# Decoder, cross-attention and FFN on one core: merged maxima, a later context load, and MLP tiles ahead of the context turn

## The reference, cut to what matters

```python
for i in range(4):                                   # decoder layers, x is 8 x 256 x 256
    x = x + self_attention(layer_norm(x), Wq, Wk, Wv, Wo, bo)   # 4 local softmax heads, 4 causal linear heads
    h = layer_norm(x)
    x = x + gelu(h @ W1 + b1) @ W2 + b2
x = _layernorm(x_in + x)
# cross-attention to ctx (8 x 120 x 256): the mask leaves query i only key i, so the softmax is 1 at that key
x = _layernorm(x + (ctx row i, or the mean row past 120) @ Wv @ Wout + bout)
# FFN with composed weights: W = sum over the top 32 of 64 pairs of w_k * A_k @ B_k
x = _layernorm(x + gelu(x @ W1c) @ W2c)
```

## Time and profile before

| | us |
|---|---|
| median of 3 runs (lowest to highest) | 958.88 (958.85 to 959.15) |
| the profiled execution's own time | 958.88 |
| its span | 957.0 |
| PE busy | 944.3 (99%) |
| DVE busy | 672.8 (70%) |
| ACT busy | 612.4 (64%) |
| POOL busy | 480.0 (50%) |

### The profile page before, as it was taken

One profiled execution on the slowest core, in us unless ns is written; L12 is line 12 of the kernel. 1 busy time (PEld: TensorE's weight loads), 2 busy tenths in 40 slices (PEclk: granted clock), 3 DMA queues, 4 the chain that ended last, 5 costly groups with the idle time before them and its releaser, 6 DMA issues.

```text
span 957.0 us, 21341 instructions
## 1 busy us (share of the span) xinstructions
PE 944.3 (99%) x8394; PEld 815.4 (85%) x8394; DVE 672.8 (70%) x1531; ACT 612.4 (64%) x1387; POOL 480.0 (50%) x381
## 2 busy tenths in 40 slices
PE   7999999999999999999999999999999999999998
PEld 4687888888888889888888888888997889998997
DVE  7696868677677868696777668776662676766445
ACT  3777777786867867777778676786856345444220
POOL 3437365456836472776466366816247224006453
PEclk9999999999999999999999999999999999999999
DMA  6221000001110000021000002000028597720001
GB/s 211 88 91 45 2 17 2 4 15 51 40 45 18 2 1 18 1 89 45 8 11 2 18 2 82 6 2 7 2 57 203 135 203 147 177 50 1 23 23 45
DMA packets 71582, 47.56 MB, mean 50 GB/s; under 512 B 44511, under 2 KB 68159, under 8 KB 71487
## 3 DMA queue, kind: packets, MB, share of 16 engines
q1 hardware_dynamic: 71487, 46.27, 18.6%
HBM read 44.16 MB, written 2.10 MB: 48 GB/s over the span
## 4 chain that ended last, share of the span: by engine, by line
PE 94%; DVE 4%; ACT 1%; issue 1%; DMA 1%; POOL 0%; SPq 0%; POOLq 0%; DVEq 0%; ACTq 0%
PE F L1464 21%; PE F L1618 19%; PE A L1464 16%; PE A L1805 5%; PE A L1798 5%; PE A L1563 4%; PE A L1958 4%; PE A L1521 3%; PE A L1580 2%; PE A L1478 2%; PE F L1478 2%; PE F L1457 2%; PE A L1554 1%; PE A L1457 1%; PE A L1537 1%; PE A L1674 1%
## 5 line engine op out<-in xcount | busy, mean ns | idle before, releaser
L1464 PE MATMUL F<-xt,w 128*128 128x512 f32 x864 | 217.8, 400 | 0.2 <-ACT scratch L1221 0.2
L475 POOL TENSOR_TENSOR ht<-scratch,ht 128x512 fp32r<-128x512 f32 x128 | 176.0, 1396 | 29.4 <-ACT ht L1224 27.9
L1464 PEld LDWEIGHTS F<-xt,w 128*128 128x128 f32 x864 | 157.6, 188 | 38.2 <-issue 3.0
L1618 PE MATMUL F<-w,ht 128*128 128x256 f32 x1536 | 188.8, 282 | 0.0
L1618 PEld LDWEIGHTS F<-w,ht 128*128 128x128 f32 x1536 | 182.8, 188 | 5.3 <-issue 4.6
L463 POOL TENSOR_TENSOR rstd<-var,minus_half 128x4 f32<-128x4 f32 x32 | 37.6, 1174 | 178.8 <-DVE var L611 178.1
L1221 ACT ACTIVATE scratch<-F,b_now 128x512 f32<-128x512 f32 x128 | 87.7, 685 | 36.6 <-POOL ht L475 19.1
L1464 PE MATMUL A<-wa,xt 128*128 128x512 f32 x372 | 89.8, 397 | 0.0
L470 POOL TENSOR_TENSOR x<-x,vec_f 128x1024 f32<-128x1024 f32 x16 | 38.0, 2376 | 94.0 <-DVE scratch L631 94.0
L1224 ACT ACTIVATE ht<-scratch 128x512 fp32r<-128x512 f32 x128 | 81.1, 634 | 4.0
L1464 PEld LDWEIGHTS A<-wa,xt 128*128 128x128 f32 x372 | 69.0, 188 | 15.9 <-issue 0.2
(11 more groups left out here) (264 smaller groups left out, 2040.3 us busy)
## 6 DMA issues: line engine op xcount, KB each, us to landing
raw_f<-in_L_attn_W_dram SPq DMA_DIRECT2D x8, 1024.0 KB, 5.5
scratch<-in_L_ffn_fc_B_dram SPq DMA_DIRECT2D x32, 256.0 KB, 4.4
scratch<-in_L_ffn_fc_A_dram SPq DMA_DIRECT2D x32, 256.0 KB, 3.9
raw_f<-in_L_ffn_fc_A_dram SPq DMA_DIRECT2D x32, 64.0 KB, 3.2
scratch<-in_x_dram SPq DMA_DIRECT2D x1, 2048.0 KB, 11.0
raw_f<-in_L_ffn_fc_B_dram SPq DMA_DIRECT2D x32, 64.0 KB, 3.2
x<-in_x_dram SPq DMA_DIRECT2D x3, 512.0 KB, 3.7
out_dram<-x SPq DMA_DIRECT2D x3, 512.0 KB, 2.9
```

Of the source, the lines that this page charges most:

```text
L475: pool.tensor_tensor(ht[:, 1, m, :], hf[:, m % 2, :], ht[:, 0, m, :].bitcast(F32), ALU.subtract).then_inc(h_lo, 1)
L1464: last = pe.matmul(out, lhs(a, c), rhs(b, c), start=clear and k == 0, stop=k == len(total) - 1, skip_group_check=not clear)
L1618: last = pe.matmul(F[:, t % 2, 0:D], ht[:, a, c, P * t:P * t + P], w2[:, b, c, :], start=k == 0, stop=k == len(passes) - 1)
```

## The change

It has three parts. (1) `dve_max` makes one reduce over four heads for each window, two instead of four for each batch; the second carries the semaphore, and ACT waits once ahead of all eight exponentials. (2) The load of the context moves in SP's list from ahead of the load of `bout` to behind the wait for the last `pe_wo`, and its target moves from `raw_a` to scratch columns 0 to 2047. (3) In step 16 PE runs `y(0)` and `y(1)` ahead of the context turn and `y(2)`, `y(3)` behind it. This `y(0)` waits for the low chunks one at a time.

```diff
-        ctx_raw = raw_a[0:NKV, :, :].rearrange("p c n -> p (c n)").rearrange("p (b n) -> p b n", b=B)
+        ctx_raw = scratch[0:NKV, 0:2048].rearrange("p (b n) -> p b n", b=B)
...
-            sp.wait_ge(wa_ready, DEPTH)
-            sp.wait_ge(wo_ready, DEPTH)
-            sp.dma_start(ctx_raw, ctx_in.rearrange("b t d -> t b d")).then_inc(ctx_loaded, 16)
             sp.wait_ge(biased[0], 4 * DEPTH)
             sp.wait_ge(ln_ready[0], TILES * ITEMS * DEPTH)
...
             sp.wait_ge(w2_ready, DEPTH)
             sp.wait_ge(wo_psum, 8 * DEPTH)
+            sp.dma_start(ctx_raw, ctx_in.rearrange("b t d -> t b d")).then_inc(ctx_loaded, 16)
             sp.wait_ge(index_ready, 1)
...
-            for h in (0, 2):
-                dve.tensor_reduce(smax[:, b, 0, h:h + 2], A[:, 2 + h:4 + h, 0:P], AX_X, ALU.min)
-                dve.tensor_reduce(smax[:, b, 1, h:h + 2], A[:, 2 + h:4 + h, P:3 * P], AX_X, ALU.min).then_inc(smax_done, 1)
+            dve.tensor_reduce(smax[:, b, 0, :], A[:, 2:6, 0:P], AX_X, ALU.min)
+            dve.tensor_reduce(smax[:, b, 1, :], A[:, 2:6, P:3 * P], AX_X, ALU.min).then_inc(smax_done, 1)
...
+            act.wait_ge(smax_done, 2 * n + b + 1)
             for h in range(NH):
-                if h % 2 == 0:
-                    act.wait_ge(smax_done, 4 * n + 2 * b + h // 2 + 1)
...
         def pe_y(pe, n, t, l):
+            by_part = t == 0 and n == ITEMS * DEPTH - 2
             if t == 0:
-                pe.wait_ge(h_lo, H_LO_0 + FC * n + FC)
+                if not by_part:
+                    pe.wait_ge(h_lo, H_LO_0 + FC * n + FC)
...
             for k, (c, a, b) in enumerate(passes):
+                if by_part and (a, b) == PASSES[0]:
+                    pe.wait_ge(h_lo, H_LO_0 + FC * n + c + 1)
...
                 else:
+                    y(0)
+                    y(1)
                     context()
-                    for t in range(TILES):
-                        y(t)
+                    y(2)
+                    y(3)
```

## The result

| | before | after |
|---|---|---|
| median, us (lowest to highest) | 959.01 (958.85 to 959.18), 4 runs | 965.61 (964.82 to 966.05), 4 runs |
| span of the profiled execution, us | 957.0 | 963.8 |
| mean granted clock of TensorE | 1.0 | 0.996 |

The changed kernel is slower: its time is 1.0064 of the one before, with a 95% interval of 1.0049 to 1.0079. By the medians that is 6.6 us, by the ratio 6.1. The forecast was 960.8 us with a range up to 963.0, so it had the sign and missed the size.

A forecast was written before the change was run, and what follows sets the result against it. PE was taken to bound the kernel, with 94% of the chain. 1.4 (stand before the context turn) + 0.4 (maxima) + 0.1 (step 0) = 1.9 us on 958.88 gave 960.8 us, range 959.0 to 963.0.

The forecast's parts named there:

- what bounds the kernel: Whole kernel: PE holds 94% of the chain, so an edit counts only where PE stands or stops standing.
- the price of the load: Context load after the last pe_wo: landing 7.0 us (5.3 to 10.4), PE standing 1.4 us (0 to 4.8) before the turn.
- 4.8 for the moving part: Context load: 4.8 us of moving once engines are free, from W2's landing at 595.44 to its own at 600.23.
- 1.7 for the fixed part: Context load: fixed part of 1.7 us, taken from the smallest landing, for 128 KB.
- 0.5 for the loads behind: Context load: 0.5 us more for the first FFN loads queued right behind it.
- the maxima: Merged reduces: exponentials 0.79 us late, covered except in steps 5, 9, 13, where PE stands 0.13 each, 0.4 in all.
- The rival with the busy queue: Context load: FFN loads share the engines, landing say 9 us, second FFN tile late; 963.2 us, chance 0.15.
- The upper bound of the forecast, 0.9: Maxima in the short steps: with the 0.94 shift, 3 x 0.28 + 3 x 0.0 = 0.9 us.
- The third rival: Maxima exceed cover: short steps cost 0.3 to 0.5 each, eleven others 0.05 to 0.1; about 962.2 us, chance 0.15.
- covered by a hair: Steps 3, 7, 11: 0.87 us of cover against exponentials 0.79 late, so no stand.
- Steps 0 and 1: First two steps, where PE waits: 0.1 us late in step 0 (minus 0.3 to 0.4), 0 in step 1.
- The rival with no stand: Context load moves like Wout, lands at 709.9 before PE needs it; only part 1's 0.5 left, 959.4 us, chance 0.2.

The follow-up runs named there:

- e3_order_only: Kernel before with only the new order y(0), y(1), context turn, y(2), y(3), load at its old place: 958.97 us, ratio 0.9998.
- e5_load_alone: Changed kernel with SP waiting for the context's landing before issuing the FFN loads: ran once, time not compared; landing took 7.9 us.
- e4_filler: Changed kernel with 15 matmuls on constants between y(1) and the context turn: 962.93 us, ratio to before 1.0044.
- e7_early_issue: Changed kernel with the context load issued behind the wait for the last pe_pv instead of the last pe_wo: 960.29 us, ratio to before 1.0014.
- e2_without_max: Changed kernel with the four reduces and two waits of the kernel before: 963.88 us, ratio to before 1.0043.
- e11_112_alone: Changed kernel loading 112 partitions, SP waiting, then 8, waiting, then FFN loads: ran once, no time given; 112 landed within 5.93 us.
- e6_112_8: Changed kernel with the context load split into 112 partitions and then 8: 962.49 us, ratio to before 1.0044.
- e9_three_tiles: Changed kernel with y(2) ahead of the context turn too, and y_add(2) ahead of DVE's context work: 963.35 us, ratio to before 1.0053.

## Why the prediction was right or wrong

**Right: what bounds the kernel, and that the change has nothing to win there.** PE was on the path, the order alone gave 0 (`e3_order_only`), and the time went up.

**The step that failed most: the price of the load.** I put its landing at 7.0 us and the stand at 1.4; they were 8.9 and 3.3. The bounds held (5.3 to 10.4), but not the value between them, 4.8 for the moving part, 1.7 for the fixed part and 0.5 for the loads behind. The 4.8 was sound, the 1.7 was not. It is the landing of `out_dram<-x` in the earlier trace rows, which is a store. The view that those rows come from has a load of the same 128 KB with nothing around it in the queue, that of `bout`:

```profile
vec_a<-in_L_xattn_bout_dram SPq DMA_DIRECT2D x1, 128.0 KB, 2.8
```

With 2.8 the sum would have been 7.6 for the load alone, close to the 7.9 measured. In `e5_load_alone` 2.8 us go by from the issue at 705.22 until the rate passes 200 GB/s, and 5.1 are left for the rest. In the old row this start-up seems to have lain under W2's transfer, so that the difference of the two landings didn't hold it; no run shows that by itself. The addition for the FFN loads behind it was 0.5 and measures 1.0. The mechanism was right, two terms of the sum were too small.

**The step that was not there: the clock.** The forecast put what a stand does to the work behind it at nothing, without a reason. The trace of before could not give a price, as no work of PE runs at a lower clock in it, but I named neither bound nor rival for it. It was 1.8 us: with the stand filled, the tiles are back to 5.71 (`e4_filler`), and without the stand too (`e7_early_issue`).

**Why the range failed.** 960.8 + 1.9 for the stand + 1.8 for the clock + 0.8 for the maxima is 965.3, against 965.6 measured. Each of the three alone would have stayed below the upper end of 963.0 (962.7, 962.6 and 961.6), and any two of them are past it. So the clock is not the only cause: had it cost nothing, the same sum would be 963.5. The rival with the busy queue came nearest, at 963.2, and partly by luck: its 3.4 for the stand is what was measured (3.3), but its 0.4 for the FFN tile did not come, as ACT copied the MLP input right behind PE's turn (724.69), and it has no clock.

**The maxima: right in place, too small in size.** I said 0.4 for steps 5, 9 and 13. By the first scores of one step and the next they lose 0.36, 0.39 and 0.44 in the changed kernel, 1.2 in all. The shift was to be 0.65 there, since DVE was "busy right through from the first batch's maxima". So it was before, but only just. The operation behind the first maxima, `y_add(0)`, needs PE's `y(0)`, which begins at 226.18 before and at 226.39 now, and it starts 3.19 us after that in both (229.37 and 229.58). So DVE's 0.14 is lost in that wait, the second maxima start no sooner (237.05 against 236.83, with PE 0.21 late), and the full 0.8 meets 0.52 of cover: 0.29 at `pe_pt` and 0.07 more by `pe_h`. The upper bound of the forecast, 0.9, had nearly this shift (0.94 - 0.14) by another way, a reduce of 1.36 us that measured 1.21, and what was measured lies above it. The third rival had 0.3 to 0.5 for each of these steps, which is the right size, from the same wrong reduce or an ACT without slack. Steps 3, 7 and 11, "covered by a hair", lose 0.13, 0.06 and 0.04, which I had at 0; the eight steps with more cover lose nothing (0.01 in all).

**Steps 0 and 1: right for 0, not for 1.** From the first scores of step 0 to those of step 1 it is 25.28 us against 25.18, late by the 0.1 that was said. Step 1, put at 0, is shorter: 45.15 us from its first scores to those of step 2, against 45.30 to 45.38 in the four kernels that have the four reduces there. Why it wins 0.15 to 0.2 is open. So the two steps together cost nothing.

**The rival with no stand fell.** Its landing was to be under 5.6 us, and it was 7.9 alone and 8.9 in the kernel. The Trainium skill (DMA: Bandwidth & Descriptors, "Anatomy of one DMA") led there too, with an estimated 4.3 us by a fit for another path than SP's; these runs don't agree with it. The 112 partitions landed within 5.9 us and the 120 in 7.9. The Trainium skill (the same page, section "Why a DMA increments its semaphore by 16 and not by 1") has a load use the largest number of engines up to 16 that divides the partitions, so 15 for 120 and 16 for 112. The direction agrees, but an estimate from these counts of that page is 7% more time for each byte with 15 engines than with 16, and 24% more was measured. The count of engines no run here shows. The granted clock stood at 0.50 in whole microseconds behind stands (715 to 718 in the profile of `e2_without_max`) and at 1.00 with the filler. The Trainium skill (TensorE: Matmul & The Clock Gate, section "What's actually happening") lists two states, 1.2 and 2.4 GHz, and says that activity releases the throttle; the trace agrees.

## What to carry to other kernels

A load that is moved close to its consumer must be priced as a lone load of its own shape, start-up included, and issued as soon as the last reader of its target is done: the wait for the last `pe_pv` in place of the last `pe_wo` gave back all 5.1 us. The fixed part of that price is read from a load, not from a store. A stand of PE costs more than its length where the granted clock falls behind it, so put a bound for that into the sum whenever a stand of some microseconds is forecast. And before a merged operation's win is handed on to the next one in the queue, look whether something between them waits for another engine; merging halves the signals too, and the consumer that started on the first half pays for it.

## What the runs showed of the hardware

- In the profiles, PE stood 3.2 to 3.3 us in three kernels (the changed one, without part 1, with the old target), 2.8 in `e11_112_alone` and 3.0 in `e5_load_alone` (its second long stand), and the granted clock fell to 0.50 behind each. It stood 2.27 us earlier in `e5_load_alone` and 1.7 in `e6_112_8`, and the two tiles behind took 5.7 us, the full-clock time. But behind the second stand of `e11_112_alone`, 2.34 us, it fell again, and in `e9_three_tiles` a stand of 0.71 and one of 1.67, 5.6 us apart, were followed by a granted clock of 0.66. So the length of one stand does not decide by itself. Nor does the clock fall in every execution of one kernel (`e2_without_max`).
- A load of 960 KB on 120 partitions took 7.9 us alone, 8.1 alone and issued earlier, and one of 896 KB on 112 partitions at most 5.9.
- A reduce of 1024 values from four PSUM banks takes 1.21 us; the 0.264 us for 256 more values, read from the two narrower ones, gives the same to within 0.01.
